# An attention and FFN block on one core: when block-wise work of a 32-stage pipeline is issued, and where the last pass computes low parts and row masks

## Chip, cores, metric

The kernel runs on one core of one Trainium2 chip. The metric is the time of one execution in microseconds, as the device measures it; the median of several executions is compared.

## What is computed

The input `x` is 64 x 32 x 512. Cut to what matters (`T` below counts 16 tiles of 128 rows, 4 batches each):

```
att   = softmax(mlp(cond))                      # 8 experts
h     = einsum(agg_w(att), x) + agg_b(att)      # mixes the 32 rows of a batch: the "mixing tiles"
proj  = h @ in_proj_w.T                         # gate, x|B|C, dt
xBC   = silu(causal_conv4(x|B|C))
dt_p  = softplus(dt + dt_bias);  dA = exp(-exp(A_log) * dt_p)      # the "step sizes" and "rates"
state = state * dA_t + dt_p * x_t B_t;  y_t = state C_t            # over 32 rows, 64 heads, 8 groups
y     = rmsnorm_per_group(y + D*x) * norm_weight * silu(gate)
x     = x + y @ out_proj_w.T
z     = grouped_conv9(x) + context
rows, cols = (softmax(z @ centroids.T / 0.1) > 0.01).any(...)      # rows kept, clusters kept
x     = x + where(rows & cols[assignments], z @ W.T + b, 0)
```

## The kernel before

**Precision.** Every large product is made of three products in fp32r: a factor is split into a high part (a rounding copy) and a low part (what the rounding left). The names end in `h` and `l`: `xh`, `xl` (activations), `wh`, `wl` (projection weights), `oh`, `ol` (output weights), `yh`, `yl` (scan output). The high part is ScalarE's in all cases. The low part is VectorE's for `xl` and `ol`, GpSimd's for `wl` and `yl`. A plain fp32 product runs as several instructions per call.

**Stages and slots.** The state-space part is 32 stages `n`: half of the tokens, group (8), and one of two blocks of 512 tokens. A stage has ten slots `m`. In each, TensorE runs one projection `proj(n,m)` of 12 matmuls 128x512; slots 0 and 1 give B and C, 2 to 5 four tiles of x, 6 to 9 four tiles of the gate. The engines work by order written out by hand: each has its own `stage(n)` (lines 571, 820, 1113, 1372) that says what it issues in which slot, and semaphores (`wait_ge`) tie them together. An engine's instructions run in the order in which they are issued, so one that waits holds up all behind it.

Around the projections TensorE runs, for stage n: `turn_x` in slot 7 (transposes of x), `Y(n,0)` and `Y(n,1)` in slot 9 and `Y(n,2)`, `Y(n,3)` in slot 2 of stage n+1 (the scan as masked products), `O(n,i)` in slots 1, 3, 4 and 5 of stage n+1 (the output projection) and `S` behind them (sums of squares). VectorE runs the three shifted adds of the convolution (`taps`, line 1041), `decays` (a scan that needs the rates, which come back from DRAM by a DMA), `scale_turned` (`dtx`, line 1061), `decayed` (`Mb` in `big`, line 1071), `y_out` (lines 1085 and 1092), `variance`, `add_out` (1110) and `split_o_lo` (1029, slots 6 to 9 of even stages). ScalarE runs `evac`, `silu`, `scale_x`, `y_square`, `y_high` and the high parts.

**Once per block of 512 tokens** (four blocks, `BLOCK_AT = {0: 1, 15: 2, 16: 3}`; block 0 is made ahead of stage 0) comes:
- mixing: operands on VectorE (`mix_operands`, 955 and 958), `mix_tile` on TensorE (413, 416), `mixed_hi` on ScalarE (729), `mixed_lo` on VectorE (967), for tiles 4b to 4b+3. TensorE runs them in slots 2 to 5 of the stage;
- step sizes: `dt_product(b)` (428 to 432) in slot 8; `dt_lower` on ScalarE (738), `dt_summed` on VectorE (984) and `dt_first` on ScalarE (743 to 746: Relu, Abs, Exp) in slot 9; then `dt_series`, twelve dependent steps on VectorE (992 to 1016), the log of the softplus as a series, all twelve in slot 4 of the next stage (in stage 0, for block 0, four in each of slots 1 to 3); `rates_exp` on ScalarE (750), `first_rates` on GpSimd (1347), a store of the rates to DRAM, and `dt_turn` with `dt_turned` in slot 6. Exp and SiLU need different function tables, which ScalarE loads when the function changes (`ACT_TABLE_LOAD`).

In stage 0 TensorE also runs `G_all(0)` (501) in slot 2 and `context` (568) in slot 5; VectorE runs `side_inputs` (971 to 978) and a copy into `diag` in slot 6; GpSimd runs `mixing_weights(2)` and `(3)` (1333, 1338) in slots 2 and 4. `x_lo` counts the low parts of mixed tiles: a wait for `x_lo, 7` is for tile 7.

**The last pass** (behind stage 31, `END`) runs the remaining `O`, `S`, the convolution (`conv2`, 617), turns of tiles (`turn`, 629) and the FFN (`ffn`, 650) in steps. Near its end VectorE thresholds the clusters (`csel`, 1321), two products (704, 705) spread them over 512 columns into two PSUM banks, VectorE selects by one of them for 12 tiles, and GpSimd, behind its six `late_base` (1398 to 1404), finishes four tiles with a copy of the other (`rows`, 934).

SyncE issues all DMAs in one queue.

## Time and profile before

| | us |
|---|---|
| median of 3 executions | 1548.5 (1547.95 to 1549.09) |
| the profiled execution | 1547.89 |
| its span, first to last instruction | 1546.1 |
| TensorE busy | 1516.0 (98%) |
| VectorE busy | 1114.8 (72%) |
| ScalarE busy | 751.2 (49%) |
| GpSimd busy | 656.7 (42%) |
| mean granted clock of TensorE | 0.994 |

In the profile's rows PE is TensorE, DVE VectorE, ACT ScalarE, POOL GpSimd; L462 is a line of the kernel before. `out<-in` are the program's names, several of them parts of one tile (`big`, `PS` above all). An entry "<-DVE vr L1100" behind an idle time names what ended the wait. A timeline row begins with the start and the duration in us; rows of equal kind that follow each other are merged (x3).

### The profile page before, as it was taken

How to read it: one execution, taken by the hardware profiler on the slowest of the kernel's cores; microseconds unless marked ns; L12 is line 12 of the kernel's file. 1: busy time of each engine (PE TensorE's matmuls, PEld its weight loads, DVE VectorE, ACT ScalarE, POOL GpSimd, SP SyncE). 2: the span in 40 equal slices, each digit the busy share in tenths (PEclk: the TensorE clock that was granted, in tenths of full speed). 3: DMA queues.
4: the chain of work that ended last, by engine and by line, in shares of the span. 5: the costliest groups of instructions: out<-in, count | busy, mean ns of one | idle time of the engine just before them, and what ended most of it. 6: DMA issues, size and time to landing. Idle time of an engine off the chain costs nothing. (4 is left out here: it accounts for less than half of the span.)

```text
span 1546.1 us, 31966 instructions
## 1 busy us (share of the span) xinstructions
PE 1516.0 (98%) x12839; PEld 1243.0 (80%) x12839; DVE 1114.8 (72%) x1725; ACT 751.2 (49%) x1302; POOL 656.7 (42%) x687
## 2 busy tenths in 40 slices
PE   8999999999999999999999999999999999999997
PEld 6778888888888888888877888888888888888687
DVE  6877767767777777777877767777777767777567
ACT  4654445454454445454564544545454544544442
POOL 4443544435253544434343352544434352543406
PEclk9999999999999999999999999999999999999999
DMA  6120212122120212111023221112121121113212
GB/s 221 60 71 23 83 35 69 56 57 67 49 66 18 81 37 69 55 56 55 9 68 124 56 69 49 52 31 77 42 69 55 56 69 48 50 32 102 93 37 109
DMA packets 57843, 97.71 MB, mean 63 GB/s; under 512 B 9120, under 2 KB 17824, under 8 KB 57696
## 3 DMA queue, kind: packets, MB, share of 16 engines
q1 hardware_dynamic: 57696, 95.67, 20.7%
q8 instruction: 102, 1.67, 0.5%
q14 instruction: 45, 0.37, 0.1%
HBM read 86.73 MB, written 8.91 MB: 62 GB/s over the span
## 5 line engine op out<-in xcount | busy, mean ns | idle before, releaser
L462 PE MATMUL PS<-xh,wh 128*128 128x512 f32 x1280 | 520.6, 407 | 0.7 <-DVE xl L967 0.6
L1041 DVE SCALAR_TENSOR_TENSOR cb<-PS,P,cb 128x496 f32<-128x496 f32 (+2 forms) x576 | 412.7, 717 | 128.8 <-ACT cb L772 115.0
L462 PE MATMUL PS<-xh,wl 128*128 128x512 f32 x1280 | 502.7, 393 | 0.0
L462 PE MATMUL PS<-xl,wh 128*128 128x512 f32 x1280 | 502.5, 393 | 0.0
L1343 POOL TENSOR_TENSOR wl<-rw,wh 128x512 fp32r<-128x512 f32 x160 | 206.1, 1293 | 221.4 <-ACT wh L717 207.5
L1353 POOL TENSOR_TENSOR ysum<-yq 128x256 f32<-128x256 f32 x128 | 112.6, 879 | 418.4 <-ACT yq L812 417.0
L462 PEld LDWEIGHTS PS<-xh,wl 128*128 128x128 f32 x1280 | 241.7, 189 | 52.6
L462 PEld LDWEIGHTS PS<-xh,wh 128*128 128x128 f32 x1280 | 242.1, 189 | 51.8 <-issue 1.3
L462 PEld LDWEIGHTS PS<-xl,wh 128*128 128x128 f32 x1280 | 242.1, 189 | 45.5
L772 ACT ACTIVATE cb<-PS,P 128x512 f32<-128x512 f32 x192 | 148.2, 772 | 179.4 <-PE PS L462 179.3
L560 PE MATMUL PS<-oh,yh 128*128 128x512 f32 x512 | 200.2, 391 | 2.5 <-issue 0.9
L560 PE MATMUL PS<-oh,yl 128*128 128x512 f32 x512 | 199.9, 390 | 0.0
L560 PE MATMUL PS<-ol,yh 128*128 128x512 f32 x512 | 199.2, 389 | 0.0
L812 ACT ACTIVATE yq<-y 128x512 f32<-128x512 f32 x128 | 81.0, 633 | 227.3 <-DVE y L1085 216.0
L779 ACT ACTIVATE big<-PS 128x512 f32<-128x512 f32 x128 | 76.2, 596 | 195.3 <-PE PS L462 194.0
L1110 DVE SCALAR_TENSOR_TENSOR acc<-PS,rs,acc 128x512 f32<-128x512 f32 x128 | 93.1, 749 | 89.4 <-issue 45.9
L794 ACT ACTIVATE big<-cb 128x512 f32<-128x512 f32 x192 | 119.6, 623 | 52.0 <-DVE cb L1041 51.7
L1085 DVE TENSOR_TENSOR y<-PS,big 128x512 f32<-128x512 f32 x128 | 87.7, 685 | 74.7 <-PE PS L522 74.7
L1370 POOL TENSOR_TENSOR rs<-vr,mh 128x1 f32<-128x1 f32 (+1 forms) x95 | 56.9, 599 | 160.6 <-DVE vr L1100 160.5
L1071 DVE TENSOR_TENSOR big<-Lt,gmt 128x512 f32<-128x512 f32 x128 | 116.7, 953 | 0.0
L560 PEld LDWEIGHTS PS<-oh,yh 128*128 128x128 f32 x512 | 96.1, 188 | 23.5 <-ACT yh L818 2.5
L560 PEld LDWEIGHTS PS<-oh,yl 128*128 128x128 f32 x512 | 96.1, 188 | 20.1
(189 smaller groups left out, 1861.2 us busy)
## 6 DMA issues: line engine op xcount, KB each, us to landing
rw<-in_w_in SPq DMA_DIRECT2D x160, 256.0 KB, 2.7
ro<-in_w_out SPq DMA_DIRECT2D x64, 256.0 KB, 3.1
dab<-rates SPq DMA_DIRECT2D x128, 128.0 KB, 3.2
x2s<-acc SPq DMA_DIRECT2D x16, 256.0 KB, 3.0
out_x<-acc SPq DMA_DIRECT2D x16, 256.0 KB, 2.5
acc<-in_x SPq DMA_DIRECT2D x3, 1024.0 KB, 10.1
wh<-x2s SPq DMA_DIRECT2D x8, 256.0 KB, 3.7
wl<-x2s SPq DMA_DIRECT2D x8, 256.0 KB, 4.6
```

Of the source, the lines that this page charges most:

```text
L462: mm = e.matmul(PS[:, proj_bank(n, m), :], w[:, m, 128 * k:128 * k + 128], v[:, k, a:a + 512], start=(i == 0), stop=(i == 11))
L560: mm = e.matmul(PS[:, O_bank(n, i), :], v[:, r, 128 * j:128 * j + 128], w[:, j, :], start=(q == 0), stop=(q == 11))
L772: e.activation(cb[:, z % 2, :], PS[:, proj_bank(n, m), :], ACT.Identity, bias=P[:, P_CB + c:P_CB + c + 1], scale=P[:, P_CW + 4 * c + 3:P_C ...
L779: e.activation(gate[:, m - 6, :], PS[:, proj_bank(n, m), :], ACT.Silu).then_inc(evac_ok.sem, 1)
L794: e.activation(dst, cb[:, (6 * n + m) % 2, :], ACT.Silu).then_inc(silu_ok.sem, 1)
L812: e.activation(yq[:, :], y[:, i % 2, :], ACT.Square).then_inc(yq_ok.sem, 1)
L1041: e.scalar_tensor_tensor(out=cv[:, :, d:32], in0=pv[:, :, 0:32 - d], scalar=P[:, P_CW + 4 * c + 3 - d:P_CW + 4 * c + 4 - d], in1=cv[:, :, ...
L1071: e.tensor_tensor(Mb[:, i % 2], bc(Lt[:, :].rearrange("p (h i t) -> p h i t", h=8, i=4)[:, :, i:i + 1, :], 128, 8, 2, 32), bc(gmt[:, i, :] ...
L1085: e.tensor_tensor(y[:, r, :].rearrange("p (j q t) -> p j q t", j=4, q=2), PS[:, PY[0]:PY[0] + 2, 256 * r:256 * r + 256].rearrange("p q (j ...
L1110: e.scalar_tensor_tensor(out=acc[:, T, :], in0=PS[:, O_bank(n, i), :], scalar=rs[:, i:i + 1], in1=acc[:, T, :], op0=ALU.mult, op1=ALU.add) ...
L1343: e.tensor_tensor(wl[:, m, :], rw[:, q % RW, :], f(wh[:, m, :]), ALU.subtract).then_inc(w_lo.sem, 1)
L1353: e.tensor_tensor(ysum[:, :], yq[:, 0:256], yq[:, 256:512], ALU.add).then_inc(ys1.sem, 1)
```

## The change

Its parts, by engine:

1. **Mixing tiles** a slot earlier: TensorE, ScalarE and VectorE handle them in slots 1 to 4. Their operands move with them (tile 4b+2's to slot 9 of the stage before, tile 4b+3's to slot 3; tile 4's ahead of the first `taps`).
2. **Step sizes**: `dt_product(b)` goes from slot 8 to slot 5 and now always into bank `PT`; `dt_lower`, `dt_first` and `dt_summed` go from slot 9 to slot 6. `turn_x(n,1)` waits for `dt_summed`, and no longer `Y(n,0)`.
3. **Series**: five steps in slot 8 and three in slot 9 of the block's own stage, the last four in slot 4 of the next. Stage 0 still runs block 0's in slots 1 to 3.
4. **Stage 0**: `G_all(0)` goes to slot 4, `G_mask(0)` and the copy into `diag` to slot 5, `context` to slot 6, `side_inputs` to slot 9, `mixing_weights(3)` on GpSimd from slot 4 to slot 3.
5. **Last pass**: the four low parts `yl` move from GpSimd to VectorE (`last_low`); GpSimd does the power for tiles 0 and 1 ahead of the sum of tile 3; `x3_low(0)` goes ahead of two `add_out`; `S(END,(2,3))` ahead of `turn(0)`; on ScalarE the biases of tile 2 go ahead of the square of tile 3.
6. **Row masks**: both factors of the products at 704 and 705 are put into fp32r tiles (`csel` in `xb`, `ohf` in `wds`), so that each is one pass. Both hold only 0 and 1.

The core of the diff:

```diff
-        pmx, csel = gmt[:, 2, :], dab[0:64, 0:128]
+        pmx, csel = gmt[:, 2, :], xb[0:64, 0:128]
...
-        asi, asf, ohf = Lt[0:64, 512:1024].bitcast(I32), y[0:64, 1, :], Lt[0:64, 0:512]
+        asi, asf = Lt[0:64, 512:1024].bitcast(I32), y[0:64, 1, :]
+        ohf = wds[0:64, :, :, :].rearrange("p k s c -> p (k s c)")
...
         def D_bank(b):
-            return PY[0] if b else PT
+            return PT
...
                 if b:
-                    pe.wait_ge(dtx_ok, ({1: 0, 2: 15, 3: 16}[b], 1))
+                    pe.wait_ge(d_sum, (b - 1, 1))
...
-                    if b is not None and 2 <= m <= 5:
-                        mix_tile(4 * b + m - 2, n)
-                    if m == 2:
-                        if n:
-                            Y(n - 1, 2)
-                            Y(n - 1, 3)
+                    if b is not None and 1 <= m <= 4:
+                        mix_tile(4 * b + m - 1, n)
+                    if n and m == 2:
+                        Y(n - 1, 2)
+                        Y(n - 1, 3)
+                    if m == (2 if n else 4):
                         G_all(n)
-                    if n == 0 and m == 5:
+                    if n == 0 and m == 6:
                         context()
...
+                    if m == 5 and b is not None:
+                        dt_product(b)
                     if m == 7:
                         turn_x(n, 0)
                         turn_x(n, 1)
-                    if m == 8 and b is not None:
-                        dt_product(b)
...
             S(END, (0, 1))
             O(END, 2)
             O(END, 3)
+            S(END, (2, 3))
             turn(0)
-            S(END, (2, 3))
...
-                    if b is not None and m == 9:
+                    if b is not None and m == 6:
                         dt_lower(b)
...
-                    if b is not None and 2 <= m <= 5:
-                        mixed_hi(4 * b + m - 2)
+                    if b is not None and 1 <= m <= 4:
+                        mixed_hi(4 * b + m - 1)
...
+            def last_low(i):
+                dve.wait_ge(y_hi, (END, i))
+                e.tensor_tensor(yl[:, i % 2, :], ygb[i % 2], f(yh[:, i % 2, :]), ALU.subtract).then_inc(y_lo.sem, 1)
...
-                    if b is not None and 2 <= m <= 5:
-                        mixed_lo(4 * b + m - 2)
+                    if b is not None and 1 <= m <= 4:
+                        mixed_lo(4 * b + m - 1)
                     if n == 0 and 1 <= m <= 3:
                         dt_series(0, 4 * m - 4, 4 * m)
+                    if b is not None and m in (8, 9):
+                        dt_series(b, *((0, 5), (5, 8))[m - 8])
                     if n - 1 in BLOCK_AT and m == 4:
-                        dt_series(BLOCK_AT[n - 1], 0, 12)
+                        dt_series(BLOCK_AT[n - 1], 8, 12)
```

What the moves make of the order on an engine, at three places. TensorE in stage 0, from the end of slot 4 or 5 on (L462 and L463 are the projections; `wds` is `dt_product`, `big` is `G_all`, `y,Lt` is `context`). Before:

```order
L413 MATMUL PS<-ab,xb 128x512
L416 MATMUL PS<-bd,acc 128x128 x4
L568 MATMUL PS<-y,Lt 128x64 x4
L462 MATMUL PS<-xh,wh 128x512
L462 MATMUL PS<-xl,wh 128x512
```

and now:

```order
L463 MATMUL PS<-xh,wh 128x512
L463 MATMUL PS<-xl,wh 128x512
L463 MATMUL PS<-xh,wl 128x512
L429 MATMUL PS<-xh,wds 128x512
L431 MATMUL PS<-xl,wds 64x512 x4
L433 MATMUL PS<-xh,wds 128x512 x3
L463 MATMUL PS<-xh,wh 128x512
```

Behind slot 5's projection stood the last mixing tile (ahead of `context`); now `dt_product(1)` stands there, with the projections of slots 6 to 9 behind it.

VectorE in stage 0, from the scan `decays` in slot 7 (`Lt<-dab,diag`) to the first `y_out`. Before:

```order
L1024 SCALAR_TENSOR_TENSOR Lt<-dab,diag 128x1024
L1029 SCALAR_TENSOR_TENSOR ol<-ro,P,oh 128x512
L1061 TENSOR_TENSOR dtx<-PS,dtt 128x512 x2
L1071 TENSOR_TENSOR big<-Lt,gmt 128x512 x2
L1029 SCALAR_TENSOR_TENSOR ol<-ro,P,oh 128x512
L984 TENSOR_TENSOR da<-PS,pb 64x256 x2
L1029 SCALAR_TENSOR_TENSOR ol<-ro,P,oh 128x512
L1085 TENSOR_TENSOR y<-PS,big 128x512
```

and now, from the same third `ol` on:

```order
L1029 SCALAR_TENSOR_TENSOR ol<-ro,P,oh 128x512
L989 TENSOR_SCALAR da<-pb 128x256
L999 RECIPROCAL dr<-da 128x256
L1001 TENSOR_TENSOR da<-pb,dr 128x256
L1003 TENSOR_TENSOR pb<-da 128x256
L1005 TENSOR_SCALAR dr<-pb 128x256
L968 TENSOR_TENSOR w<-y,C 128x96
L970 TENSOR_TENSOR yq<-PS,C 128x256
L973 TENSOR_REDUCE yq<-yq 128x64
L975 TENSOR_TENSOR cxb<-yq,P 128x64
L1029 SCALAR_TENSOR_TENSOR ol<-ro,P,oh 128x512
L1007 SCALAR_TENSOR_TENSOR dr<-dr,pb 128x256 x3
```

`dt_summed` (`da<-PS,pb`) has left, eight steps of the series and the four instructions of `side_inputs` have come in ahead of `y_out`.

ScalarE in slot 6 of stage 16, from the evacuation of the gate's first tile (`big<-PS`). Before:

```order
L779 ACTIVATE big<-PS 128x512
L756 COPY dtt<-PS 128x2x2x64
L794 ACTIVATE big<-cb 128x512
L804 ACTIVATE big<-big,P 128x512 x2
L724 ACTIVATE oh<-ro,P 128x512
L779 ACTIVATE big<-PS 128x512
```

and now:

```order
L734 COPY pb<-PS 64x512
L775 ACTIVATE big<-PS 128x512
L752 COPY dtt<-PS 128x2x2x64
L790 ACTIVATE big<-cb 128x512
L739 ACTIVATE pb<-da,P 128x256
L740 ACTIVATE da<-da,P 128x256
L742 ACT_TABLE_LOAD
L742 ACTIVATE pb<-da 128x256
L800 ACTIVATE big<-big,P 128x512 x2
L721 ACTIVATE oh<-ro,P 128x512
L775 ACT_TABLE_LOAD
L775 ACTIVATE big<-PS 128x512
```

The high part `oh`, on which VectorE's second `ol` waits, now stands behind the exponential and a table load; a second load follows it.

## Rows read from the trace of the kernel before

**Rows 1.** The page, part 1: busy time of each engine.

```profile
PE 1516.0 (98%) x12839; PEld 1243.0 (80%) x12839; DVE 1114.8 (72%) x1725; ACT 751.2 (49%) x1302; POOL 656.7 (42%) x687
```

**Rows 2.** Waits of TensorE, whole span: us in total, times, longest us.

```profile
PE PS L541 <- DVE vr L1100: 4.5, 2, 2.3
PE PS L489 <- ACT big L794: 3.0, 1, 3.0
PE PS L501 <- ACT big L794: 2.6, 1, 2.6
...
PE PS L428 <- DVE dtx L1061: 1.2, 1, 1.2
```

**Rows 3.** TensorE by stretches: length, busy (instructions), granted clock, DMA share, GB/s.

```profile
818.00:822.50 4.50, 4.47 (x14) 0.62 0.14 29
```

**Rows 4.** Timeline of VectorE in stage 0, series steps.

```profile
30.51 1.22 DVE L992 TENSOR_SCALAR da<-pb 128x256 f32<-128x256 f32 x1
...
34.01 1.50 DVE L1004 TENSOR_TENSOR pb<-da 128x256 f32<-128x256 f32 x1
...
39.45 2.83 DVE L1008 SCALAR_TENSOR_TENSOR dr<-dr,pb 128x256 f32<-128x256 f32 x3
...
46.77 0.35 DVE L1016 TENSOR_SCALAR da<-dr,scol 128x256 f32<-128x256 f32 x1
```

**Rows 5.** Timeline of ScalarE in stage 0.

```profile
31.55 1.15 ACT L794 ACTIVATE big<-cb 128x512 f32<-128x512 f32 x2
...
47.16 0.42 ACT L750 ACTIVATE pb<-da 128x256 f32<-128x256 f32 x1 [5.78 <-DVE da L1016]
...
50.60 0.57 ACT L729 CAST xh<-PS 128x512 fp32r<-128x512 f32 x1
```

**Rows 6.** Timeline of GpSimd in stage 0.

```profile
33.95 1.28 POOL L1343 TENSOR_TENSOR wl<-rw,wh 128x512 fp32r<-128x512 f32 x1 [2.37 <-ACT wh L717]
```

**Rows 7.** Timeline of TensorE: `Y(0,0)` with `Y(0,1)`, and `O(0,0)`.

```profile
66.84 1.16 PE L522 MATMUL PS<-big,dtx 64*64 64x64 f32 x64
...
73.51 0.39 PE L560 MATMUL PS<-oh,yh 128*128 128x512 f32 x1
```

**Rows 8.** Timeline of VectorE: the first `y_out`.

```profile
68.07 0.69 DVE L1085 TENSOR_TENSOR y<-PS,big 128x512 f32<-128x512 f32 x1 [1.58 <-PE PS L522]
```

**Rows 9.** Timeline of GpSimd: the first `y_low`.

```profile
71.90 1.29 POOL L1362 TENSOR_TENSOR yl<-yg,yh 128x512 fp32r<-128x512 f32 x1
```

**Rows 10.** Timeline of ScalarE: the first `y_square`.

```profile
69.97 0.62 ACT L812 ACTIVATE yq<-y 128x512 f32<-128x512 f32 x1
```

**Rows 11.** Timeline of VectorE in stage 16: steps 1, 4 and 9.

```profile
761.23 0.28 DVE L992 TENSOR_SCALAR da<-pb 128x256 f32<-128x256 f32 x1
...
763.80 0.42 DVE L1004 TENSOR_TENSOR pb<-da 128x256 f32<-128x256 f32 x1
...
765.97 0.42 DVE L1010 SCALAR_TENSOR_TENSOR pb<-dr,pb 128x256 f32<-128x256 f32 x1
```

**Rows 12.** Timeline of ScalarE: `dt_first(3)`, slot 9 of stage 16.

```profile
785.72 0.50 ACT L744 ACTIVATE da<-da,P 128x256 f32<-128x256 f32 x1
786.24 1.28 ACT L746 ACT_TABLE_LOAD   x1
```

**Rows 13.** Timeline of TensorE in stage 17.

```profile
818.03 0.35 PE L541 MATMUL PS<-C,big 128*128 128x1 f32 x2 [2.23 <-DVE vr L1100]
...
833.60 1.30 PE L522 MATMUL PS<-big,dtx 64*64 64x64 f32 x64 [1.00 <-DVE big L1071]
```

**Rows 14.** Timeline of VectorE in the last pass: the last two `add_out`.

```profile
1466.67 1.41 DVE L1110 SCALAR_TENSOR_TENSOR acc<-PS,rs,acc 128x512 f32<-128x512 f32 x2 [0.86 <-issue]
```

**Rows 15.** Timeline of TensorE: the first row mask.

```profile
1529.42 1.12 PE L704 MATMUL PS<-Lt,dab 64*128 64x512 f32 x2 [1.56 <-DVE dab L1321]
```

**Rows 16.** Timeline of GpSimd: end of `late_base(15)`, start of `finish_apart(0)`.

```profile
1530.56 1.28 POOL L1404 TENSOR_TENSOR dtx<-dtx,acc 128x512 f32<-128x512 f32 x1
1532.10 1.27 POOL L1411 TENSOR_TENSOR big<-big,y 128x512 f32<-128x512 f32 x1 [0.27 <-ACT y L934]
```

More of the change, by code:

```diff
@@ L840, in stage @@
                         dt_first(0)
-                    if b is not None and m == 9:
-                        dt_first(b)
                     if m == 6 and n in TURNED:
@@ L850, in stage @@
                         y_high(n - 1, 3)
+                    if b is not None and m == 6:
+                        dt_first(b)
                     if m == 6:
@@ L915, in scalar_program @@
             x3_biased(1)
-            for i in (2, 3):
-                y_high(END, i)
-                y_square(END, i)
+            y_high(END, 2)
+            y_square(END, 2)
+            y_high(END, 3)
             x3_biased(2)
+            y_square(END, 3)
             x3_biased(3)
@@ L998, in dt_series @@
                         dve.wait_ge(d_step, (b, k - 1))
+                        if k == 1 and b:
+                            dve.wait_ge(DT_ok, b - 1)
                         if k == 1:
@@ L1117, in stage @@
                         dt_summed(0)
+                    if n == 0 and m == 0:
+                        mix_operands(4)
                     if n == 0 and m < 6:
@@ L1164, in stage @@
                         decayed(n, 1)
-                    if b is not None and m == 9:
+                    if b is not None and m == 6:
                         dt_summed(b)
@@ L1303, in vector_program @@
             variance(END, (2, 3))
+            x3_low(0)
             add_out(END, 2)
             add_out(END, 3)
-            x3_low(0)
             dve.wait_ge(ld_as)
@@ L1387, in stage @@
                         split_w_lo(0, m + 4)
+                    if n == 0 and m in (2, 3):
+                        mixing_weights(m)
                     if n and m == 3:
@@ L1391, in stage @@
                         split_w_lo(n // 2 + 1, m)
-                    if n == 0 and m in (2, 4):
-                        mixing_weights(1 + m // 2)
             def late_base(T):
@@ L1422, in gpsimd_program @@
                 stage(n)
-            for i in (0, 1):
-                y_low(END, i)
-            for i in (0, 1):
-                y_sum(END, i)
-            for i in (2, 3):
-                y_low(END, i)
-            for i in (2, 3):
+            for i in (0, 1, 2):
                 y_sum(END, i)
             rstd(END, (0, 1))
+            y_sum(END, 3)
             for k in (0, 1):
```

30 lines of the change are left out of this document (15 added, 15 removed).

## The prediction

> **What bounds the kernel now.** I read the page first: TensorE is busy 1516.0 us of a span of 1546.1 [rows 1]. No other engine comes near, so only idle or slowed time of TensorE can be won, and work on another engine costs something only where TensorE waits for it. The list of TensorE's waits comes next [rows 2]: the largest are few and single. 2.6 us ahead of the products `G_all(0)`, 3.0 us ahead of `turn_x(0)`, 4.5 us in two waits of the row sums `S` for a variance, 1.2 us of `dt_product(3)` for `dtx`. After each wait of over 2 us TensorE's granted clock sits at its lower level (1.2 instead of 2.4 GHz) for a while: in the 4.5 us behind one of them the mean is 0.62, which is 4.5 x 0.38 = 1.7 us lost [rows 3]. Waits of 1.0 and 1.2 us were not followed by this. I charge 1.6 us for each wait over 2 us. So the stalls that the change aims at hold some 20 us, 6 of them slow clock. The sum is made against the profiled execution, 1547.9 us, which lies 0.6 below the median of the three runs, 1548.5; the same difference is then put on the median.
>
> **Stage 0, slots 1 to 5.** Mixing tiles now come a slot earlier, `G_all(0)` two slots later, and `dt_product(1)` moves from slot 8 to slot 5. `G_all(0)` then finds its input ready: its 2.6 us and the slow clock go. But `dt_product(1)` needs `x_lo(7)`, the low part of the last mixing tile, and TensorE's queue behind it holds all of slots 6 to 9. When does `x_lo(7)` come? Today the twelve series steps end at 46.77 + 0.35 = 47.1 us [rows 4]; ScalarE answers with `rates_exp` at 47.16, and its slot 4 list ends with the copy of a tile at 50.60 + 0.57, so 4.05 us behind the series [rows 5]. In the change that list ends with tile 7, and VectorE's subtraction takes 0.6: `x_lo(7)` = end of series + 4.8. The series itself ends later: VectorE now waits for tile 4's high part between `taps(0,1)` and the first step. Today the first step starts at 30.51; ScalarE begins its first SiLU at 31.55, behind a table load, and then copies tile 4 by 32.7 [rows 5], so 2.1 us of idle, plus one more low part ahead of the last steps (0.6), less `G_mask` (0.3): 47.1 + 2.4 = 49.5 at today's contention. That contention is visible: step 1 took 1.22 us and step 4 1.50 [rows 4], where undisturbed ones take 0.28 and 0.42 [rows 11]; step 4 ended at 35.51, just behind the GpSimd instruction that ran beside it till 35.23 [rows 6]. With all of it gone the end would be 47.2, with one more blocked step 50.5; I take 48.7, between them and nearer to today's. Then `x_lo(7)` is at 53.5. TensorE reaches `dt_product(1)` at about 44 to 45.5 (it also waits 1 to 3 us for the operands of tile 7, which VectorE makes behind `taps(0,2)`; the sum doesn't hang on this), so **a stall of 8 to 9 us** takes the place of the two old ones. From there: product 1.84, three projections with what lies between them 2.85 + 0.45 + 0.9 + 2.85 + 1.25 + 2.85, the last projection 2.73, `Y(0)` 1.1, in all 16.8, and 1.6 for the slow clock: `Y(0,1)` ends at 71.9. Today it ends at 66.84 + 1.16 = 68.0 [rows 7]. **+3.9 us** (bounds +2.4 and +5.7 from the two ends of the series).
>
> **Stage 0 to 1.** `y_out(0,0)` starts 0.07 us behind `Y(0,1)` today, at 68.07 [rows 8], and `O(0,0)` starts at 73.51, 5.5 us behind [rows 7]. The chain between (add, square, two sums, low part on GpSimd) ends at 71.90 + 1.29 = 73.2 [rows 9], 5.1 us long; 1.2 of this is ScalarE's, whose square starts at 69.97 and not at 68.76, since the exponentials stand in front [rows 10]. Without them it is 3.9, so VectorE may be 1.6 us late, not more. Now it gets, ahead of `y_out(0,0)`, eight series steps: 765.97 - 761.23 = 4.74 us undisturbed [rows 11], the side inputs moved from slot 6 (1.75), and it waits in slot 7: `split_o_lo(0,1)` needs ScalarE's `oh`, and ScalarE's slot 6 now holds two copies, the load of the exponential's table and the exponential [rows 12] in front of it, 2.5 us in all. Counted on from the end of `dt_product(1)` (E): decays till E+6.5, `oh` at E+8.9, turned and decayed products E+12.1, three low parts 2.1, series and side inputs 6.5, which makes E+20.0, against `Y(0,1)` at E+15.0: 5.0 late. `O(0,0)` then waits 5.0 + 3.9 - 5.5 = 3.4, and the clock falls, 1.6 more: **+5.0 us** (bounds 1.5 and 6.5).
> ScalarE: Activation LUTs of the Trainium skill (section What ACT_TABLE_LOAD costs) speaks against this part: a switch of tables costs some 2.66 us there, half of it a drain. Here the load starts 0.02 us behind the instruction before it and takes 1.28 [rows 12], so I count 1.3; by the page `oh` would come 1.4 us later at both places where slot 6 holds it, and the sum would be 2.8 us higher.
>
> **Stage 1, stage 17.** There the twelve steps stood in slot 4, ahead of the variance: `S` waited 2.25 and 2.23 us, and `Y` 1.0 us because the rates came late [rows 2, 13]. Eight of twelve steps, 4.7 us, are gone from slot 4, where `S` was late by 2.2; the rates leave as much earlier. Both waits go in both stages: -(2.2 + 1.6 + 1.0) = **-4.8 us, twice**. Their cover is VectorE's idle time in stages 0, 15 and 16, which is what the neighbouring terms charge.
>
> **Stage 15 to 16.** No low parts of `oh` here, but `dt_product(2)` has left slot 8, so `Y(15,1)` comes 1.8 us sooner behind the turns while VectorE has 4.7 more to do, beside GpSimd's `split_w_lo`. `y_out(15,0)` about 3 us late; the mixing product ahead of `O(15,0)` gives 1.0 back, so `O` waits 0.4 where it waited 0.85; `mix_tile(13)` waits some 1.3 for `x_lo(12)`. **+0.9** (0 and +3).
>
> **Stage 16 to 17.** As stage 0 to 1 without the side inputs: `y_out(16,0)` 4.2 late, `O(16,0)` waits 4.2 + 3.9 - 5.5 = 2.6, slow clock 1.6, less the 1.2 of `dt_product(3)` [rows 2]: **+3.0** (bounds -1.2 and +4.5).
>
> **Last pass.** `x3_low(0)` goes ahead of two `add_out` (1.41 us) and fills the 0.86 us in which VectorE waited ahead of them [rows 14]; `add_out(END,0)` no longer waits for two sums on GpSimd; `S(END,(2,3))` is done before `turn(0)`. Low parts on VectorE take 0.7 each instead of 1.3 to 1.7 on GpSimd, but stand in its queue ahead of `dtx`: +0.7 at `O(END,0)`. Net, the first FFN product starts 1.6 us sooner (0.9 to 2.1). The row masks: the first of two products took 1.12 us, as two instructions of full precision [rows 15], the second as long; in one pass each I take 0.4, so some 1.3 less. But GpSimd, which `rows` releases, is busy until 1531.84 with `late_base(15)` and starts 0.26 later [rows 16]: the end gains 0.2. Net **-1.8**.
>
> **Sum:** 3.9 + 5.0 - 4.8 + 0.9 + 3.0 - 4.8 - 1.8 = +1.4; 1547.9 + 1.4 = 1549.3 for the profiled execution, 1549.9 for the median. The change moves waits rather than ending them. What a measurement can tell from no change is about 0.2%, 3.1 us.
>
> **Rivals.**
> Forecast, no change that can be told (1545.4 to 1551.6): 0.40.
> Faster: the y chain is not late. If ScalarE's slot 6 list and VectorE's eight steps fit into the idle time that stages 0 and 16 show, neither `O(0,0)` nor `O(16,0)` waits: 5.0 and 4.2 us drop out, 1549.9 - 9.2 = 1540.7, and with half of it 1545. It decides at 1.6 us: `y_out` less late than this behind `Y`. For it: VectorE waits for `Y(0)` ahead of `y_out` today [rows 8]; against it: the 4.74 + 1.75 of work that goes in. 0.28.
> Slower: VectorE's steps are blocked by GpSimd for whole instructions. In stage 0 GpSimd's `mixing_weights(2)` and `(3)` now run back to back beside steps 3 to 12, and in stage 15 `split_w_lo` beside steps 3 to 8. Step 4's 1.50 us is the price of one such meeting, 1.1 over its own time [rows 4]. The series of stage 0 then ends at 50.5 (+1.8), stage 15 loses 1.5, `mix_tile(13)` as much: 1549.9 + 4.8 = 1554.7. It decides from a series end of 50 us on. 0.32. SBUF — State Buffer of the Trainium skill (section SBUF: two separate sides) has this as a rule: a VectorE operation with two SBUF inputs and a reading GpSimd operation lock each other out for a whole instruction. Steps 1 and 4 agree; two of the three steps merged at 39.45 did not wait beside GpSimd's strided adds, which speaks against its holding everywhere.
> That the masks are no single pass: 0.2 us more, inside the forecast.
>
> **Numbers.** Likeliest 1549.9. The range takes in the slower case and most of the faster one: 1543.0 to 1556.0. Faster 0.28, same 0.40, slower 0.32.
>
> **What would show it.** One TensorE wait of 8 to 9 us ahead of `dt_product(1)`, on `xl`; `Y(0,1)` ending near 72; `O(0,0)` waiting over 2 us for `yl` with the clock low behind it; no wait of `S` for `vr` in stages 1 and 17; the turn of tile 1 no later than 1.5 us before today's distance from the end. I am wrong if `dt_product(1)` waits under 5 us, or if `O(0,0)` and `O(16,0)` start without a wait.

## Result, and the profile after

The changed kernel takes **1552.2 us** (median of 20 runs, 1551.1 to 1553.5); the kernel before took 1549.5 in the same sitting (20 runs, 1546.5 to 1555.0). The ratio is 1.0021, with a 95% interval of 1.0015 to 1.0027: slower by 2.7 us by the medians and 3.2 by the ratio, right at the 0.2% that part "no change" from "slower" in the prediction. Its range holds the result; its time was 2.3 us low. One term, stage 0, was 5.6 us too small, and errors of the other sign hid more than half of that.

| | before | after |
|---|---|---|
| median of 20 runs | 1549.5 us | 1552.2 us |
| profiled execution (its span) | 1547.9 (1546.1) us | 1552.2 (1550.4) us |
| first projection of stage 0 starts | 18.75 us | 19.81 us |
| TensorE's waits of over 0.3 us from there to slot 9 of stage 0 | 2.6 + 3.0 | 0.4 + 5.7 + 7.3 |

The third row has nothing to do with the change. In the thirteen profiles of this study, one of each kernel, the first projection starts between 18.73 and 20.65 us; in that of `last_pass_alone`, whose start is that of the kernel before, at 20.34. In the profile of after, six matmuls that only keep TensorE busy took 2.93 us instead of 1.65: single ones last 0.63 us there and 0.39 in before, as they do at the lower and the higher clock elsewhere. So 1.1 of the 4.3 us by which the two spans differ is the start, and 3.2 are left, as by the ratio.

Busy time has not moved [rows 1]:

```profile
PE 1516.2 (98%) x12837; PEld 1243.8 (80%) x12837; DVE 1118.5 (72%) x1729; ACT 751.3 (48%) x1302; POOL 656.1 (42%) x683
```

The waits of TensorE have. This is the list for the whole span (us in total, times, longest), against [rows 2]:

```profile
PE PS L429 <- DVE xl L964: 7.3, 1, 7.3
PE PS L414 <- issue: 6.1, 2, 5.7
PE PS L557 <- POOL yl L1374: 4.8, 2, 2.6
...
PE PS L557 <- DVE dtx L1061: 1.4, 1, 1.4
...
PE PS L414 <- DVE dtx L1061: 1.0, 1, 1.0
...
PE PS L414 <- DVE xl L964: 0.9, 1, 0.9
```

L429 is `dt_product`, L414 a mixing tile, L557 the output products `O`. All four waits shown in [rows 2] are gone: `S` for the variance, `turn_x(0)`, `G_all(0)` and `dt_product(3)`. In their place stand three kinds of new ones: 5.7 and 7.3 us in stage 0, 2.6 and 2.3 at `O(0,0)` and `O(16,0)`, and 1.0 and 0.9 at two mixing tiles of stage 16. The places themselves, from TensorE's timeline:

```profile
45.34 0.77 PE L414 MATMUL PS<-ab,xb 128*128 128x512 f32 x1 [5.69 <-issue]
...
59.73 0.80 PE L429 MATMUL PS<-xh,wds 128*128 128x512 f32 x1 [7.27 <-DVE xl L964]
...
77.39 1.16 PE L519 MATMUL PS<-big,dtx 64*64 64x64 f32 x64
78.48 0.50 PE L463 MATMUL PS<-xh,wh 128*128 128x512 f32 x1
...
86.78 0.47 PE L557 MATMUL PS<-oh,yh 128*128 128x512 f32 x1 [2.56 <-POOL yl L1374]
...
801.79 0.77 PE L557 MATMUL PS<-oh,yh 128*128 128x512 f32 x1 [2.25 <-POOL yl L1374]
```

`Y(0,1)` ends at 77.39 + 1.16 = 78.55, where it ended at 68.0 [rows 7].

To see where time goes I laid the two timelines over each other and read, at the first product of a stage's (or slot's) projection, how late TensorE is against the trace of before:

| first product of | late by, us | part | measured | predicted |
|---|---|---|---|---|
| stage 0 | +1.06 | start, chance | +1.1 | 0 |
| stage 1 | +10.55 | stage 0 | **+9.5** | +3.9 |
| stage 1, slot 2 (behind `O(0,0)`) | +13.39 | stage 0 to 1 | +2.8 | +5.0 |
| stage 2 | +8.16 | stage 1 | -5.2 | -4.8 |
| stage 17 | +7.98 | stages 15 and 16 | -0.2 | -0.3 (0.9 less the 1.2 of `dt_product(3)`) |
| stage 17, slot 2 (behind `O(16,0)`) | +12.04 | stage 16 to 17 | +4.1 | +4.2 |
| stage 18 | +6.81 | stage 17 | -5.2 | -4.8 |
| end of the span | +4.3 | last pass | -2.5 | -1.8 |
| sum | | | +4.4 | +1.4 |

(The +4.4 is off 4.3 by rounding.) Six terms of seven lie within 2.2 us, most within 0.7. Stage 0 is 5.6 off. VectorE's timeline there shows why; compare [rows 4]:

```profile
35.70 0.69 DVE L964 TENSOR_TENSOR xl<-PS,xh 128x512 fp32r<-128x512 f32 x1 [2.10 <-ACT xh L726]
36.31 0.28 DVE L989 TENSOR_SCALAR da<-pb 128x256 f32<-128x256 f32 x1
...
39.06 2.45 DVE L1003 TENSOR_TENSOR pb<-da 128x256 f32<-128x256 f32 x1
41.43 2.21 DVE L1041 SCALAR_TENSOR_TENSOR cb<-PS,P,cb 128x496 f32<-128x496 f32 x3
...
43.89 1.35 DVE L955 TENSOR_TENSOR ab<-xb,C 128x128 fp32r<-128x128 f32 x1
...
45.76 1.83 DVE L1005 TENSOR_SCALAR dr<-pb 128x256 f32<-128x256 f32 x1
47.63 2.76 DVE L1007 SCALAR_TENSOR_TENSOR dr<-dr,pb 128x256 f32<-128x256 f32 x3
...
54.56 0.35 DVE L1015 TENSOR_SCALAR da<-dr,scol 128x256 f32<-128x256 f32 x1
...
58.98 0.69 DVE L964 TENSOR_TENSOR xl<-PS,xh 128x512 fp32r<-128x512 f32 x1 [0.70 <-ACT xh L726]
```

and GpSimd beside it (L1345 and L1350 are `mixing_weights(2)` and `(3)`, L1355 a subtraction of `split_w_lo`):

```profile
38.70 2.53 POOL L1345 TENSOR_TENSOR big<-big 128x1024 f32<-128x1024 f32 x1
...
43.78 1.31 POOL L1355 TENSOR_TENSOR wl<-rw,wh 128x512 fp32r<-128x512 f32 x1
45.06 2.39 POOL L1345 TENSOR_TENSOR big<-big 128x1024 f32<-128x1024 f32 x1
47.53 2.02 POOL L1350 TENSOR_TENSOR big<-big 128x512 f32<-128x512 f32 x2
49.63 0.48 POOL L1350 TENSOR_TENSOR AW<-big 128x128 f32<-128x128 f32 x1
```

Step 4 of the series ends at 41.51, behind the instruction that ends at 41.23; tile 7's operand at 45.24, behind 45.09; step 5 at 47.59, behind 47.45. The series ends at 54.91, and 4.8 us later (59.67) comes `x_lo(7)`, exactly the distance that the prediction gave. So the chain behind the series was right. The end of the series was not: 54.91 is 6.2 us behind the predicted 48.7, of which 1.1 is the later start of this execution. Counted from the first projection it is 35.1 us instead of 29.95, 5.1 too late.

### The profile page after: what moved, and what is told of

Same layout as the page of the kernel before. It is cut to its first block and busy times, and to the rows that moved or that the text cites. A ratio compares the mean times of both kernels' runs of the same rounds, so it can differ in the third digit from the quotient of the medians.

```text
span 1550.4 us, 31966 instructions
## 1 busy us (share of the span) xinstructions
PE 1516.2 (98%) x12837; PEld 1243.8 (80%) x12837; DVE 1118.5 (72%) x1729; ACT 751.3 (48%) x1302; POOL 656.1 (42%) x683
## 5 line engine op out<-in xcount | busy, mean ns | idle before, releaser
L463 PE MATMUL PS<-xh,wh 128*128 128x512 f32 x1280 | 519.3, 406 | 0.6 <-DVE xl L964 0.6
L1041 DVE SCALAR_TENSOR_TENSOR cb<-PS,P,cb 128x496 f32<-128x496 f32 (+2 forms) x576 | 412.7, 716 | 127.3 <-ACT cb L768 113.5
L463 PE MATMUL PS<-xh,wl 128*128 128x512 f32 x1280 | 501.3, 392 | 0.0
L463 PE MATMUL PS<-xl,wh 128*128 128x512 f32 x1280 | 501.2, 392 | 0.0
L1355 POOL TENSOR_TENSOR wl<-rw,wh 128x512 fp32r<-128x512 f32 x160 | 209.6, 1315 | 227.0 <-ACT wh L714 212.3
L463 PEld LDWEIGHTS PS<-xh,wh 128*128 128x128 f32 x1280 | 241.4, 189 | 51.3 <-issue 1.0
L463 PEld LDWEIGHTS PS<-xh,wl 128*128 128x128 f32 x1280 | 240.7, 188 | 52.0
L463 PEld LDWEIGHTS PS<-xl,wh 128*128 128x128 f32 x1280 | 241.4, 189 | 45.1
L557 PE MATMUL PS<-oh,yh 128*128 128x512 f32 x512 | 201.2, 393 | 6.5 <-POOL yl L1374 4.8
L557 PE MATMUL PS<-oh,yl 128*128 128x512 f32 x512 | 200.6, 392 | 0.0
L557 PE MATMUL PS<-ol,yh 128*128 128x512 f32 x512 | 200.0, 391 | 0.0
L557 PEld LDWEIGHTS PS<-oh,yh 128*128 128x128 f32 x512 | 96.5, 189 | 28.1 <-issue 8.2
L1071 DVE TENSOR_TENSOR big<-Lt,gmt 128x512 f32<-128x512 f32 x128 | 113.0, 924 | 0.0
L557 PEld LDWEIGHTS PS<-oh,yl 128*128 128x128 f32 x512 | 96.5, 188 | 20.2
```

Source lines behind the costliest of these rows:

```text
L463: mm = e.matmul(PS[:, proj_bank(n, m), :], w[:, m, 128 * k:128 * k + 128], v[:, k, a:a + 512], start=(i == 0), stop=(i == 11))
L557: mm = e.matmul(PS[:, O_bank(n, i), :], v[:, r, 128 * j:128 * j + 128], w[:, j, :], start=(q == 0), stop=(q == 11))
L1041: e.scalar_tensor_tensor(out=cv[:, :, d:32], in0=pv[:, :, 0:32 - d], scalar=P[:, P_CW + 4 * c + 3 - d:P_CW + 4 * c + 4 - d], in1=cv[:, :, ...
L1071: e.tensor_tensor(Mb[:, i % 2], bc(Lt[:, :].rearrange("p (h i t) -> p h i t", h=8, i=4)[:, :, i:i + 1, :], 128, 8, 2, 32), bc(gmt[:, i, :] ...
L1355: e.tensor_tensor(wl[:, m, :], rw[:, q % RW, :], f(wh[:, m, :]), ALU.subtract).then_inc(w_lo.sem, 1)
```

## Experiments

The theory, **A**: stage 0 holds the whole loss. VectorE's instructions there are held by GpSimd, the series ends late, and TensorE waits for `x_lo(7)` at its new place. The rivals: the parts of the change hang together (B); VectorE's lateness comes of its own queue and of ScalarE, and GpSimd only fills the gap. Each kernel was timed in five rounds beside the kernel before, whose medians were 1549.0 to 1549.5 us in the four sittings; differences to the changed kernel go across sittings. The intervals of the ratios are 1.3 to 2.4 us either way, and single profiles start up to 1.9 us apart; so where a part is read from a profile, it is against the start of its own stage 0.

### 1. The parts taken apart

`stage0_back`, the changed kernel with stage 0 as before:

```
-                    if b is not None and 1 <= m <= 4:
+                    if b is not None and 0 <= m - (1 if n else 2) <= 3:
...
-                    if m == 5 and b is not None:
+                    if n and m == 5 and b is not None:
                         dt_product(b)
...
+                    if n == 0 and m == 8:
+                        dt_product(b)
```

(and the same for ScalarE's, VectorE's and GpSimd's lists of stage 0, and for block 1's steps in stage 1).

> The changed kernel with all of stage 0 (and the series of tile block 1) put back as before: mixing tiles in slots 2 to 5, dt_product(1) in slot 8, all twelve steps in slot 4 of stage 1, GpSimd's mixing_weights in slots 2 and 4. Stages 15 to 17 and the last pass stay changed. Theory A (stage 0 holds the whole loss, the other parts gain and do not depend on it): against the changed kernel the +10.6 of stage 0 and +2.8 of its hand-over go, the 5.2 won in stage 1 too, and the 1.1 that the two profiles differ in ahead of the first projection is no part of it: 1552.2 - 7.1 = 1545.1 us, 0.997 of the kernel before. Rival B (the parts hang together, the gains of the later ones are only time that stage 0's lateness had made): 1548 to 1550, the same as before.

Measured: 1544.95 us (6 runs), ratio 0.9968 (0.9957 to 0.9980): 7.2 us below the changed kernel. A holds, B falls. Its profile says the same part by part: stages 15 and 16, 16 to 17, 17 and the last pass give -0.2, +4.1, -5.2 and -2.5 us here too, with stage 0 as before.

`last_pass_alone`, the kernel before with only this and the row masks, the order of `S` and ScalarE's and GpSimd's lists behind it:

```
             y_out(END, 1)
+            last_low(0)
             scale_turned(END, 2)
...
+            x3_low(0)
             add_out(END, 2)
             add_out(END, 3)
-            x3_low(0)
```

> The kernel before with only the last pass changed (low parts on VectorE, order of S and turn, row masks in one pass). Theory A: the 2.5 us that the profile of the changed kernel shows behind the last stage (TensorE +6.8 us late at stage 31, span +4.3) come from these edits alone: 1549.5 - 2.5 = 1547.0, 0.9984 of before. The prediction's own working gives 1.8: 1547.7. Rival B: the gain came from what the body left behind: 1549.5, 1.0000.

Measured: 1546.47, ratio 0.9987 (0.9978 to 0.9997). In its profile TensorE is 4.1 us late at stage 31 and 1.7 at the end: 2.5 won behind the last stage, as in the changed kernel. The gain belongs to these edits; which of them won it, no run separates. Of the 4.1, 1.6 are the start; 2.7 come in slot 8 of stage 16, in code that was not touched:

```profile
782.56 0.80 PE L429 MATMUL PS<-xh,wds 128*128 128x512 f32 x1 [2.45 <-DVE dtx L1063]
```

It is `dt_product(3)`, which waited 1.2 us in the profile of before [rows 2], with the granted clock at 1.00 behind it. Here it waited 2.45, and the clock was 0.66 over the 5 us from 782. In `before_no_late_weights`, with the same code here, it waited 1.0. So the one execution that the prediction stood on was short in its start, and a single wait can differ by 2.7 us from one execution to the next.

### 2. Who holds VectorE in stage 0

`no_late_weights`: GpSimd's mixing weights of tiles 8 to 15 are left out and zeros written in their place.

```
             def mixing_weights(c):
+                if c >= 2:
+                    for i in range(4):
+                        e.memset(AW[:, 4 * c + i, :], 0.0).then_inc(mix_pool.sem, 1)
+                    return
```

> The changed kernel, but GpSimd leaves out the mixing weights of tiles 8 to 15 and writes zeros in their place (four small memsets for each group of four tiles), so that nothing of GpSimd's runs beside series steps 3 to 9 of stage 0; the tiles of x from 8 on are mixed with weights of zero. Theory A (VectorE's steps are held by GpSimd for whole instructions: 2.45 us for step 4, 1.83 for step 5, 2.76 for three steps, 1.35 for one operand of tile 7, against 0.43, 0.29, 1.34 and 0.28 undisturbed, 6.1 us in all): the series ends at 48.5 to 50 instead of 54.9, TensorE's wait ahead of dt_product(1) shrinks from 7.3 to 1 to 3 us, the total is 5 to 6 us shorter: 1546 to 1547. Rival B (VectorE is late because its queue waits for ScalarE's copies, and GpSimd only fills the same gap): series end above 53, total within 1 us of 1552.2.

Measured: 1546.36, ratio 0.9981 (0.9972 to 0.9990): 5.8 us below the changed kernel. VectorE's timeline, the same instructions as above:

```profile
37.06 0.28 DVE L989 TENSOR_SCALAR da<-pb 128x256 f32<-128x256 f32 x1
...
39.81 0.42 DVE L1003 TENSOR_TENSOR pb<-da 128x256 f32<-128x256 f32 x1
40.16 2.21 DVE L1041 SCALAR_TENSOR_TENSOR cb<-PS,P,cb 128x496 f32<-128x496 f32 x3
...
43.29 0.28 DVE L1005 TENSOR_SCALAR dr<-pb 128x256 f32<-128x256 f32 x1
43.61 1.34 DVE L1007 SCALAR_TENSOR_TENSOR dr<-dr,pb 128x256 f32<-128x256 f32 x3
...
49.11 0.35 DVE L1015 TENSOR_SCALAR da<-dr,scol 128x256 f32<-128x256 f32 x1
```

Step 4 takes 0.42 instead of 2.45, step 5 0.28 instead of 1.83, three steps 1.34 instead of 2.76; from the first step to the end of the last it is 12.4 us instead of 18.6. The taps (L1041), which read their tile from PSUM, take 2.21 in both, GpSimd beside them or not. So the rival falls that VectorE is late through its queue and ScalarE alone. In one point the expectation missed: the wait ahead of `dt_product(1)` shrank only to 6.7 us, because TensorE came to it 5 us sooner as well: the 5.7 us wait for tile 7's operands went down to 2.5. Both waits hang on VectorE's queue. The prediction said that its sum does not hang on the first of them, which is so, but a reader of the profile who looks at the second alone would see little gained.

`before_no_late_weights`: the same in the kernel before.

> The kernel before, with GpSimd's mixing weights of tiles 8 to 15 left out and zeros in their place, as in no_late_weights. There it gave the changed kernel 5.8 us. Theory A' (these GpSimd instructions cost the kernel before next to nothing, since its two waits in stage 0, 2.6 us ahead of G_all(0) and 3.0 ahead of turn_x(0), lie behind ScalarE's SiLUs, not behind the end of the series; the change has made the series' end the thing that TensorE waits for): 0 to 1.5 us less than before, 1547.5 to 1549. Rival B' (they cost the same 6 us of VectorE's time there, and TensorE's 5.6 us of waits are their price): 1543 to 1545, both waits under 1 us.

Measured: 1546.72, ratio 0.9981 (0.9971 to 0.9991), 2.7 us (1.4 to 4.5) less: more than A' gave, much less than B'. Its timeline of TensorE:

```profile
55.53 1.21 PE L489 MATMUL PS<-C,big 64*128 64x64 f32 x32 [0.96 <-ACT big L794]
...
61.50 0.51 PE L428 MATMUL PS<-xh,wds 128*128 128x512 f32 x1 [1.79 <-DVE dtx L1061]
```

`G_all(0)` still waits 2.5 us, `turn_x(0)` 1.0 instead of 3.0, `dt_product(1)` 1.8 instead of nothing; TensorE leaves stage 0 1.9 us sooner. So the same GpSimd work cost the old kernel some 2 us in stage 0 and costs the new one 6: the change did not make the collision, it put TensorE right behind it. The old kernel's series was held for some 4 us already: step 1 for 0.9, step 4 for 1.1, step 5 for 0.5 (0.77 instead of 0.28), and 1.5 in the three single steps of the merged row at 39.45 [rows 4], where undisturbed ones take 0.42 or 0.43:

```profile
39.45 0.78 DVE L1008 SCALAR_TENSOR_TENSOR dr<-dr,pb 128x256 f32<-128x256 f32 x1
40.26 0.58 DVE L1008 SCALAR_TENSOR_TENSOR dr<-dr,pb 128x256 f32<-128x256 f32 x1
40.88 1.39 DVE L1008 SCALAR_TENSOR_TENSOR dr<-dr,pb 128x256 f32<-128x256 f32 x1
```

`operand4_behind`: one edit undone.

```
-                    if n == 0 and m == 0:
-                        mix_operands(4)
                     if n == 0 and m < 6:
                         taps(0, m)
                     if n == 0 and m == 0:
+                        mix_operands(4)
                         mix_operands(5)
```

> The changed kernel with one edit undone: the operands of mixing tile 4 are made behind taps(0,0) again, not ahead of it. Theory A: they cost 2.7 us ahead of the taps (1.29 and 1.37, held by GpSimd) and hold back SiLU, tile 4 and the start of the series; put back, the first step starts 1.5 to 2.5 us sooner and the end comes 1.5 to 2.5 sooner: 1549.7 to 1550.7. Rival B (the series then meets the same GpSimd instructions at other steps, and their end sets its end): series end within 0.5 us of 54.9, total 1552.

Measured: 1551.66, ratio 1.0015 (1.0006 to 1.0024); against the changed kernel 0.5 us, which is not to be told from nothing, so A's total was not reached. The profile tells more. In the changed kernel the two operands stand ahead of the taps and wait for GpSimd's weights:

```profile
25.05 1.29 DVE L952 TENSOR_TENSOR bd<-AW,C 128x128 f32<-128x128 f32 x1 [2.16 <-POOL AW L1350]
26.27 1.37 DVE L955 TENSOR_TENSOR ab<-xb,C 128x128 fp32r<-128x128 f32 x1
27.56 2.21 DVE L1041 SCALAR_TENSOR_TENSOR cb<-PS,P,cb 128x496 f32<-128x496 f32 x3
```

Behind the taps they no longer hold these back. The first step starts 14.45 us behind the first projection instead of 16.50, where the prediction had it; from there the series takes 18.6 us, as in the changed kernel, and ends 2.0 us sooner. TensorE leaves stage 0 2.5 us sooner against its start (+7.0 instead of +9.5). Then `O(0,0)` waits 2.6 us as before, but now the clock falls behind it (0.67 over the 5 us from 84, against 1.00 behind the same wait in the changed kernel), and 1.6 of the 2.5 are given back.

### 3. Moved waits

`series_tail_behind`:

```
-                    if n == 0 and 1 <= m <= 3:
-                        dt_series(0, 4 * m - 4, 4 * m)
+                    if n == 0 and m in (1, 2, 4):
+                        dt_series(0, *{1: (0, 4), 2: (4, 8), 4: (8, 12)}[m])
```

(and the exponential of the rates one slot later).

> The changed kernel with the last four series steps of tile block 0 moved from slot 3 to slot 4 of stage 0 (behind the low part of tile 7), and rates_exp(0) on ScalarE and first_rates(0) on GpSimd from slot 4 to slot 5. Theory A (TensorE's 7.3 us wait ahead of dt_product(1) hangs on the series, since rates_exp stands ahead of evac(0,4) and of tile 7's copy): tile 7's low part then comes behind taps(0,4) alone, at 55.9 instead of 59.7 of the span; the wait shrinks to 3.5, Y(0,1) ends 3.5 us sooner, total 1548.7. Rival B (the rates come 3 us later and the decays' scan then waits for the transfer that brings them back, 11 us behind rates_exp in stage 17): scan at 69 or later, gain under 1 us: 1551 to 1552.

Measured: 1549.34, ratio 0.9992 (0.9984 to 1.0001), 2.8 us below the changed kernel. A's link holds: the wait for `xl` is halved.

```profile
56.17 0.50 PE L429 MATMUL PS<-xh,wds 128*128 128x512 f32 x1 [3.38 <-DVE xl L964]
...
82.67 0.77 PE L557 MATMUL PS<-oh,yh 128*128 128x512 f32 x1 [3.47 <-POOL yl L1374]
```

`Y(0,1)` ends 5.2 us sooner against the start of the stage, more than expected, as the clock stays up behind the shorter wait. The second row is where part of it goes: `O(0,0)` now waits 3.5 us for the y chain, which did not come forward as far, and the clock is 0.50 over the 5 us behind it. Here B had a link right: the scan waits 1.8 us for the rates to come back. But it starts at 66.2 and not at 69, and B's total falls.

`block1_steps_back`:

```
-                    if b is not None and m in (8, 9):
+                    if n and b is not None and m in (8, 9):
                         dt_series(b, *((0, 5), (5, 8))[m - 8])
...
-                        dt_series(BLOCK_AT[n - 1], 8, 12)
+                        dt_series(BLOCK_AT[n - 1], 8 if n > 1 else 0, 12)
```

> The changed kernel, but in stage 0 no series steps of block 1 stand in slots 8 and 9: all twelve stand in slot 4 of stage 1, as before the change (blocks 2 and 3 stay spread). Theory A (the spread moves a wait rather than ending it: y_out(0,0) starts 4.2 us behind Y(0,1) through 4.7 us of steps, and O(0,0) waits 2.6 for it; in stage 1 it wins S's 2.2, the slow clock behind it and Y's 1.0): without it O(0,0) waits under 0.7 us, S in stage 1 waits 1.1 to 2.3 with slow clock behind, Y 1 to 2.7; net +1 to +3 us: 1553 to 1555. Rival E (the side inputs, 1.75 us, and ScalarE's oh make y_out late, not the steps): O(0,0) still waits over 2 us, and the total is 5 us worse, 1557.

Measured: 1553.17, ratio 1.0018 (1.0007 to 1.0029). TensorE passes `O(0,0)` with no wait of over 0.3 us, and `y_out(0,0)` starts 0.07 us behind `Y(0,1)`: taking the steps out was enough (E falls). In the changed kernel VectorE works without a pause between these two rows:

```profile
72.58 0.75 DVE L1029 SCALAR_TENSOR_TENSOR ol<-ro,P,oh 128x512 fp32r<-128x512 f32 x1 [2.34 <-ACT oh L721]
...
82.76 0.68 DVE L1085 TENSOR_TENSOR y<-PS,big 128x512 f32<-128x512 f32 x1
```

The 4.7 us of steps are the largest item of this stretch; the wait of 2.3 for `oh` ahead of it and the 1.3 of side inputs in it add to the lateness too, and no run takes these out alone. `S` in stage 1 waits 1.7 us and `Y` 1.1. The run loses nothing at `O(0,0)`, where the changed kernel loses 2.8 us, and wins 2.0 in stage 1, where that wins 5.2. So the spread of block 1 is worth 0.4 us by the profiles and 1.0 by the medians, and by the ratios (1.0018 against 1.0021) it costs 0.5: not to be told from nothing. One wait was sold for another.

### 4. Towards a better kernel

`series_3_5_4` is `stage0_back` with blocks 2 and 3 spread differently:

```
-                        dt_series(b, *((0, 5), (5, 8))[m - 8])
+                        dt_series(b, *((0, 0), (0, 3))[m - 8])
...
+                    if n >= 2 and n - 1 in BLOCK_AT and m == 3:
+                        dt_series(BLOCK_AT[n - 1], 3, 8)
```

> stage0_back with the series of tile blocks 2 and 3 spread otherwise: three steps (2.5 us) in slot 9 of stages 15 and 16 instead of eight (4.7 us) in slots 8 and 9, five in slot 3 and four in slot 4 of the next stage. Theory C (y_out behind Y may be 1.6 us late, and is 3.9 late in stage 16 through these steps; the 2.25 us wait of O(16,0) and 1.6 to 1.8 of slow clock behind it are their price, while S in stage 17 stays served, since VectorE waits 1.6 us ahead of taps(17,4) anyway): O(16,0) waits under 0.5 us, mix_tile(12) in stage 16 no longer waits for dtx (1.0): 4 to 5 us less than stage0_back's 1545.0: 1540.5. Rival D (the steps in slot 3 hold back the taps or S's variance as slot 4 did, and the wait comes back a slot later): 1544 to 1546.

Measured: 1546.11, ratio 0.9976 (0.9966 to 0.9985): no gain over `stage0_back`. `O(16,0)` waits 1.26 us and not 2.25, with the clock up, `mix_tile(12)` not at all. But the list of waits has a new first row, and VectorE's timeline in stage 17 names the cause of its longest one:

```profile
PE PS L523 <- DVE big L1077: 4.6, 2, 3.3
```

```profile
824.26 2.29 DVE L1030 TENSOR_TENSOR_SCAN Lt<-dab,diag 128x1024 f32<-128x1024 f32 x1 [5.18 <-DMA dab<-rates]
```

Neither C nor D had it: `Y(17,0)` waits 3.3 us, for decays whose rates are still on their way to memory and back. TensorE is earlier, the rates are not. (The profiled execution took 1543.8 us, 2.3 below the kernel's median, so this wait is its own and not surely that of every execution.)

`series_354_and_stage1`: the same, and in stage 1 four of block 1's twelve steps go to slot 3.

> series_3_5_4, and in stage 1 the first four steps of block 1 in slot 3, eight in slot 4, instead of twelve in slot 4. Theory C: the 3.0 us of the four steps lie beside a wait of VectorE of about 1.6 us ahead of taps(1,4); S's wait (1.1 to 2.25 us in slot 5 of stage 1) and Y's (2.7 in stage0_back) shrink by 1.6 each: 1.5 to 4 us less than series_3_5_4: 1538. Rival D: no gain, as slot 3 of stage 1 has no idle time: within 0.7 us of series_3_5_4.

Measured: 1544.46 (7 runs), ratio 0.9968 (0.9956 to 0.9980), 1.7 us below `series_3_5_4`, inside the scatter of both. `S` in stage 1 still waits 2.2 us and `Y` 1.4 + 1.0. Nothing follows from it.

`rates_in_slot4`: all of the last steps one slot earlier, and `rates_exp` with them.

```
-                    if n in TURNED and m == (5 if n else 4):
+                    if n in TURNED and m == 4:
                         rates_exp(TURNED[n])
...
+                    if n - 1 in BLOCK_AT and m == 3:
+                        dt_series(BLOCK_AT[n - 1], 3 if n > 1 else 0, 12)
```

> stage0_back with the last series steps one slot earlier and the rates with them: for blocks 2 and 3 three steps in slot 9 and nine in slot 3 of the next stage, for block 1 all twelve in slot 3 of stage 1, rates_exp and first_rates in slot 4 instead of 5. In series_3_5_4 O(16,0) waited 1.3 instead of 2.25 us, but Y(17,0) 3.3 instead of 0, since the rates' way out and back ends when it ends. Theory F (that way, from rates_exp over the transfers to the decays' scan, some 11 us, is the floor of stages 1 and 17 once the other waits are gone): rates one slot earlier end Y's waits in both, 1.3 to 2.7 us in stage 1 and 3.3 with slow clock in stage 17: 3 to 6 us less than series_3_5_4's 1546.1, so 1540 to 1543. Rival D (taps(17,4) and ScalarE's evac behind the exponential come late instead, and projections or S wait): 1545 to 1547.

Measured: 1543.19 (6 runs), ratio 0.9958 (0.9943 to 0.9974), the shortest of all: 9.0 us below the changed kernel, 6.1 below the one before. The waits of `Y` are gone from its list, whose first rows are now:

```profile
PE PS L542 <- DVE vr L1110: 4.4, 2, 3.1
PE PS L490 <- ACT big L796: 3.0, 1, 3.0
PE PS L502 <- ACT big L796: 2.5, 1, 2.5
```

The gain over `series_3_5_4` is 2.9 us, just short of F's 3 to 6, and the intervals of the two just overlap; D is half right: `S` waits more (3.1 in stage 1). That it beats `stage0_back` (by 1.8) lies within the intervals of the two. That it beats the changed kernel and the one before is clear of noise.

`weights_early`: `stage0_back` with one line added behind `split_w_lo(0, 3)` and GpSimd's `mixing_weights(2)` taken out of slot 2.

```
             split_w_lo(0, 3)
+            mixing_weights(2)
```

> stage0_back with GpSimd's mixing_weights(2) moved from slot 2 of stage 0 to ahead of it, behind split_w_lo(0,3), into GpSimd's 4 to 6 us without work, so that it no longer meets series steps 4 to 9. Theory A (what GpSimd holds back is what TensorE waits for at turn_x(0); leaving out both groups took that wait from 3.0 to 1.0 in the kernel before): the wait shrinks by 1 to 2 us: 1543 to 1544. Rival B (the same 4.9 us of GpSimd then meet the operands of tiles 4 to 6, dt_summed and the first steps, and G_all(0) waits longer): 1545 to 1547.

Measured: 1545.01, ratio 0.9967 (0.9954 to 0.9979): as `stage0_back`. B holds. TensorE's timeline:

```profile
35.84 0.60 PE L502 MATMUL PS<-big 128*32 128x32 f32 x28 [5.19 <-ACT big L796]
...
58.67 0.53 PE L490 MATMUL PS<-C,big 64*128 64x64 f32 x10 [2.42 <-ACT big L796]
```

`G_all(0)` waits 5.2 instead of 2.5, `turn_x(0)` 2.4 instead of 3.0. Moving work that holds another engine moves what is held.

## Why the prediction came out as it did

The range holds the result; the forecast case, up to 1551.6, misses it by 0.6 us. By its own test, a series end past 50 us, it is the slower rival that came true, at another price than it was given. That the total came within 2.3 us is luck: one term was far off and others gave back. Step by step:

- **Stage 0, wrong by 5.6 us** (+3.9 predicted, bounds +2.4 and +5.7; +9.5 measured). The step that failed is the end of the series: "With all of it gone the end would be 47.2, with one more blocked step 50.5; I take 48.7". It came 5.1 us later, in two parts; the rest is the 18.9 instead of 18.4 us below.
  - *3.1 us: the meetings with GpSimd.* From the first step to the last I counted 15.5 us, 0.8 less than at the old kernel's contention; it took 18.6. Without the late weights it is 12.4, so the held time is 6.2, where the old kernel had some 4. Four meetings make it, of 1.1 to 2.0 us (one is with `split_w_lo`, which the weights push there). I had the rival (VectorE "blocked by GpSimd for whole instructions"), its page and its deciding point (a series end of 50), and priced it at 1.8 us in stage 0, from one row [rows 4] where GpSimd's instruction was a 1.28 us subtraction [rows 6]. `mixing_weights` starts with a multiply over 1024 columns that takes 2.5 us. In these rows the price of a meeting is what is left of GpSimd's instruction. I also read the merged row at 39.45 wrongly: its three steps take 0.78, 0.58 and 1.39 us, so each was held, beside the strided adds too; I took 2.3 us of contention out of a series that held some 4. The rule of the Trainium skill (SBUF — State Buffer, section SBUF: two separate sides), that the one that starts first has the shared port for its whole instruction, agrees here with each of the four held rows, and in the taps, which read one operand from PSUM and took 2.21 us beside GpSimd as without it.
  - *2.0 us: not in the sum at all.* Tile 4's operands, put ahead of `taps(0,0)`, wait for GpSimd's weights and are then held; the first step starts that much later (`operand4_behind`).
  - The undisturbed end, 47.2, looks right: `no_late_weights`, less its later start of 1.7, ends at 47.7. But two errors cancel in it: its first step starts 2.1 us later than I counted, and from there it is 1.6 us shorter.
- **`x_lo(7)` = end of series + 4.8, and 18.4 us from there to `Y(0,1)`:** right; 4.8 and 18.9 measured. The wait of "8 to 9 us" was 7.3, as TensorE came late to it itself through the wait for tile 7's operands: I gave that 1 to 3 us, it was 5.7.
- **Stage 0 to 1, too high by 2.2:** `y_out(0,0)` was 4.2 us behind `Y(0,1)`, not 5.0, and `O(0,0)` waited 2.6, not 3.4. The other 1.6, slow clock, did not come in this profile, though it did behind the same wait in `operand4_behind`. As printed, the terms add to E+20.7; the 20.0 comes out because one of the three low parts is inside the E+12.1 already. That the steps are the largest part of the lateness, `block1_steps_back` shows.
- **Stages 1, 15 and 16, 16 to 17, 17:** each within 0.4 us. Both `S` waits and both `Y` waits went, `O(16,0)` took their place. In stage 16 the number is right with other parts: `O(15,0)` doesn't wait (0.4 predicted), and `mix_tile(12)` waits 1.0 us for `dtx`, which I had not.
- **Last pass, 0.7 better** than -1.8. In the trace of before TensorE waits 3.8 us in four places there, in after 1.7 in two. `last_pass_alone` gives 2.5 by its profile. The row masks:

```profile
1533.99 0.49 PE L701 MATMUL PS<-wds,xb 64*128 64x512 f32 x1 [1.58 <-DVE xb L1333]
1534.33 0.39 PE L702 MATMUL PS<-wds,xb 64*128 64x512 f32 x1
```

are single passes of 0.4 each, as taken, against two of 1.12 and more [rows 15]; from the first mask to the end of the span it is 16.4 us instead of 16.7, against the 0.2 counted; no experiment was made for it.
- **Errors of both signs met in the total.** Stage 0 at +9.5 makes 1555.5 of the forecast; the 2.2 of the hand-over, 0.7 of the last pass and 0.4 each of stages 1 and 17 bring it back to 1551.8. The measured terms without the start sum to +3.2, which is what the ratio says. The base was low too, 1548.5 from three runs where twenty give 1549.5.
- **The other rivals:** the faster one needed `O(0,0)` and `O(16,0)` without a wait; both waited. By ScalarE: Activation LUTs of the Trainium skill (section What ACT_TABLE_LOAD costs) `oh` would have come 1.4 us later than I counted. Here the load took 1.28 with no drain to be seen [rows 12], and `oh` was done at E+9.0, where E is the end of `dt_product(1)`, against E+8.9 counted without one, which speaks against it.

What stays open: why `O(16,0)` and `O(0,0)` are followed by slow clock in some executions and not in others (below).

## What to carry to other kernels

When work is moved next to another engine's, price a meeting at the full length of the other engine's longest instruction there, and count the meetings from the timelines instead of taking one for all. Read held instructions one by one against their undisturbed length: 1.5 us of held time stood in one merged row here. An operation hoisted ahead on TensorE's in-order queue should be checked against the latest end of what it reads, with that contention in it: the same GpSimd instructions cost 2 us while TensorE had other work ahead of its wait, and 6 once its wait stood right behind the series that they hold. Waits of an engine that is 98% busy are worth little singly: removing one showed the next (the y chain, then the round trip of the rates), so follow each until it is named who is late after it.
